# Four of the thirteen transfers of each half of the query stack, issued from ScalarE's queue in the steady rounds

## The reference, cut to what matters

```
q = split_heads(x @ w_q);  k, v = split_heads(text @ w_k), split_heads(text @ w_v)
k_ip, v_ip = split_heads(ip_h @ w_k_ip), split_heads(ip_h @ w_v_ip)
out = softmax(q k^T / sqrt(32)) v + softmax(q k_ip^T / sqrt(32) + mask_ip) v_ip
result = merge_heads(out) @ w_out + b_out + x
```

## Time and profile before

| what | value |
|---|---|
| median of three runs | 734.93 us (734.69 to 735.64) |
| profiled execution | 729.49 us |
| its span, first to last instruction | 727.7 us |
| TensorE busy | 688.1 us, 95% |
| VectorE busy | 540.1 us, 74% |
| ScalarE busy | 288.3 us, 40% |
| GpSimd busy | 213.5 us, 29% |
| transfers on SyncE's queue | 88.45 MB, 44.7% of 16 engines' span |
| transfers on ScalarE's queue | 0.61 MB, 0.4% |
| granted TensorE clock, mean | 0.979 of full speed |

### The profile page before, as it was taken

One profiled execution on the slowest core, in us unless ns is written; L12 is line 12 of the kernel. 1 busy time (PEld: TensorE's weight loads), 2 busy tenths in 40 slices (PEclk: granted clock), 3 DMA queues, 4 the chain that ended last, 5 costly groups with the idle time before them and its releaser, 6 DMA issues.

```text
span 727.7 us, 18922 instructions
## 1 busy us (share of the span) xinstructions
PE 688.1 (95%) x6410; PEld 628.2 (86%) x6410; DVE 540.1 (74%) x1686; ACT 288.3 (40%) x626; POOL 213.5 (29%) x359
## 2 busy tenths in 40 slices
PE   4979778999999999999999999999999999999987
PEld 3567467989999998989999999999999989899876
DVE  5341539878787979797878788787879797978764
ACT  1031117153534435261617162535444261617061
POOL 7100004324150504142423324151505042423223
PEclk9879999999999999999999999999999999999979
DMA  9935954253434444433435263534344444434310
GB/s 266 323 98 137 267 147 121 66 155 92 136 90 134 102 127 103 140 89 102 130 89 156 68 163 82 147 96 127 98 127 103 133 96 125 104 92 114 90 49 37
DMA packets 79543, 89.52 MB, mean 123 GB/s; under 512 B 10680, under 2 KB 63416, under 8 KB 79492
## 3 DMA queue, kind: packets, MB, share of 16 engines
q1 hardware_dynamic: 79016, 88.45, 44.7%
q10 hardware_dynamic: 492, 0.61, 0.4%
HBM read 39.21 MB, written 10.62 MB: 68 GB/s over the span
## 4 chain that ended last, share of the span: by engine, by line
PE 75%; DMA 8%; DVE 7%; SPq 6%; issue 2%; ACT 1%; ACTq 0%; POOL 0%; DVEq 0%
PE psum L1019 32%; PE psum L1124 9%; PE psum L1076 7%; PE psum L1108 6%; PE psum L1103 5%; DMA q_stack<-aux_a 4%; SPq L457 3%; PE psum L1132 3%; PE psum L901 3%; PE psum L1133 2%; SPq L429 2%; DMA wo_raw<-in_L_xattn_w_v_ip 2%; PE psum L1147 2%; PE psum L980 2%; PE psum L1130 1%
## 5 line engine op out<-in xcount | busy, mean ns | idle before, releaser
L522 POOL TENSOR_TENSOR attn<-o_parts 128x128 f32<-128x128 f32 x160 | 73.8, 461 | 418.9 <-DVE o_parts L844 418.9
L803 DVE TENSOR_REDUCE neg_max<-psum 128x2 f32<-128x292 f32 x320 | 144.7, 452 | 64.0 <-PE psum L1076 63.4
L1019 PE MATMUL psum<-wo_both,at_hi 128*128 128x320 f32 x640 | 153.2, 313 | 0.0
L1019 PE MATMUL psum<-xt_hi,wq_hi 128*128 128x256 f32 x400 | 114.9, 287 | 1.4 <-DVE xt_lo L773 1.4
L1076 PE MATMUL psum<-k_stack,q_stack 104*128 104x154 f32 x640 | 112.6, 286 | 3.5 <-DVE neg_max L804 1.5
L1019 PE MATMUL psum<-xt_hi,wq_lo 128*128 128x256 f32 x400 | 112.1, 280 | 0.0
L1019 PE MATMUL psum<-xt_lo,wq_hi 128*128 128x256 f32 x400 | 112.0, 280 | 0.0
L831 DVE TENSOR_TENSOR p_lo<-psum,p_hi 128x512 f16<-128x512 f32 x160 | 107.9, 682 | 2.8 <-ACT psum L657 2.8
L1019 PEld LDWEIGHTS psum<-wo_both,at_hi 128*128 128x128 f32 x640 | 109.6, 188 | 0.0
L655 ACT ACTIVATE p_hi<-psum 128x512 f16<-128x512 f32 x160 | 95.3, 595 | 27.8 <-PE psum L1103 27.7
L1124 PE MATMUL psum<-v_tail,p_tail 128*128 128x264 f32 x320 | 102.0, 400 | 2.6 <-DVE p_lo L831 1.6
(11 more groups left out here) (93 smaller groups left out, 1260.3 us busy)
## 6 DMA issues: line engine op xcount, KB each, us to landing
q_stack<-q_hi SPq DMA_DIRECT2D x128, 96.0 KB
x_in<-in_x SPq DMA_DIRECT2D x16, 640.0 KB, 4.1
x_res<-in_x SPq DMA_DIRECT2D x16, 640.0 KB, 5.1
out<-out_sb SPq DMA_DIRECT2D x32, 320.0 KB
q_stack<-q_hi SPq DMA_DIRECT2D x128, 64.0 KB
q_stack<-q_lo SPq DMA_DIRECT2D x64, 96.0 KB
q_stack<-q_lo SPq DMA_DIRECT2D x64, 64.0 KB
q_stack<-aux_a SPq DMA_DIRECT2D x48, 64.0 KB, 2.4
```

The costliest lines, as they stand in the source:

```text
L522: nc.gpsimd.tensor_tensor(cols, o_parts[:, qt, 0:4, :], o_parts[:, qt, 4:8, :], ALU.add).then_inc(att_half, 1)
L803: nc.vector.tensor_reduce(dst[:, :, 0], src[:, :, 0:TEXT], AX_X, ALU.max, negate=True)
L1019: last = nc.tensor.matmul(ps, l(c), r(c), start=(i == 0), stop=(i == len(terms) - 1))
```

## The change

The four transfers of the first part of each half (rows 0 to 31, the high part) leave SyncE's block and are issued from ScalarE's queue in all rounds that have a BACK stage. In ScalarE's list the block for set A comes behind ST(2,1) and ahead of Q3, the one for set B behind Q4 and ahead of AT(0,0). The other nine transfers stay with SyncE. All count on the same semaphore as before. In round 0 SyncE issues all thirteen.

```diff
 ACT_STEPS = [
...
-    (BACK, "ST", 2, 1), (FRONT, "Q", 3), (BACK, "ST", 3, 0), (BACK, "ST", 3, 2), (BACK, "ST", 3, 1),
-    (BACK, "ST", 4, 0), (BACK, "ST", 4, 1), (BACK, "ST", 4, 2), (FRONT, "Q", 4), (BACK, "AT", 0, 0), (NEXT, "X", 0),
+    (BACK, "ST", 2, 1), (FRONT, "STK", 0), (FRONT, "Q", 3), (BACK, "ST", 3, 0), (BACK, "ST", 3, 2), (BACK, "ST", 3, 1),
+    (BACK, "ST", 4, 0), (BACK, "ST", 4, 1), (BACK, "ST", 4, 2), (FRONT, "Q", 4), (FRONT, "STK", 1), (BACK, "AT", 0, 0),
+    (NEXT, "X", 0),
...
+        def queries_to_stack(queue, n, row, part):
+
+            groups = (SET_A, SET_B)[n]
+            g0, g1 = groups[0], groups[-1] + 1
+            src = q_hi if part == "hi" else q_lo
+            for j in range(4):
+                queue.dma_start(q_stack[row:row + DH, 4 * g0 + j:4 * g1:4, :].bitcast(F32),
+                                src[DH * j:DH * (j + 1), g0:g1, :].bitcast(F32)).then_inc(stack_in[n], 16)
...
-                        for row, part in STACK_PARTS:
-                            src = q_hi if part == "hi" else q_lo
-                            for j in range(4):
-                                sp.dma_start(q_stack[row:row + DH, 4 * g0 + j:4 * g1:4, :].bitcast(F32),
-                                             src[DH * j:DH * (j + 1), g0:g1, :].bitcast(F32)).then_inc(stack_in[n], 16)
+                        for row, part in STACK_PARTS[1:] if it.back else STACK_PARTS:
+                            queries_to_stack(sp, n, row, part)
...
+                    if kind == "STK":
+                        n = args[0]
+                        groups = (SET_A, SET_B)[n]
+
+                        act.wait_ge(qh_done, t * GROUPS + groups[-1] + 1)
+                        act.wait_ge(st_ready, t * ST_ALL - ST_ALL + 1 + max(ST_TURN[(g, u)] for g in groups for u in range(3)))
+                        queries_to_stack(act, n, *STACK_PARTS[0])
```

## The result

The changed kernel took 760.6 us (median of 4 runs, 756.0 to 764.4) against 734.8 us for the kernel before in the same comparison (4 runs, 733.0 to 735.6): ratio 1.037, 95% interval 1.031 to 1.042. It is slower, as forecast, but by 25.8 us where the sum said 14.5, and 0.6 us beyond the top of the range. The profiled execution took 759.7 us, its span is 757.9 us.

A forecast was written before the change was run, and what follows sets the result against it. TensorE was taken to bound the kernel, busy 38.50 of 38.80 us per steady round. Stalls of 11.76 + 0.62 + 0.95 + 0.71 + 0.50 = 14.5 us on the 734.93 us median gave 749 us, range 736 to 760.

The forecast's parts named there:

- the sum: Whole run: steady rounds 11.76 us, rounds 1, 8 and 15 0.62, 0.95 and 0.71, plus 0.50: 14.5 us slower.
- block 1: Set B's four ScalarE issues between Q4 and AT(0,0): wait for Q4's result, stall S(1,0,0) by 0.98 us per steady round.
- signs: Steady rounds: AT(0,0) starts 3.0 us after Q4, TensorE idles about 1 us ahead of S(1,0,0), mask waits gone.
- block 0: Set A's four ScalarE issues ahead of Q3: 2.51 us, Q3 delayed 0 to 0.15 us, covered by 0.64 us slack.
- the threshold: Between Q4 and AT(0,0) on ScalarE: the stall of S(1,0,0) begins at 0.35 us per issue.
- the price of block 1 in the sum: Behind Q4: four issues at 597 ns, 2.51 us, plus 0.05 us wait and register work; S(1,0,0) 0.98 us late.
- The price of an issue beside another queue's: SyncE and ScalarE issuing at once: larger ratio 1.7 gives 1.02 us per issue; 597 ns was taken instead.
- (B): Rival: SyncE and ScalarE issuing at once slow each other, 1.02 us per issue, 789 us, or 769 us; chance 0.10.
- (D): Rival: earlier stack arrival makes timed runs faster, about 730 us, if ScalarE issues stay under 0.35 us; chance 0.11.
- (C): Rival: no change, 735 us; ScalarE issues of 0.3 to 0.4 us fit the gap, stack not waited for; chance 0.11.

The follow-up runs named there:

- Two issues: Kernel before with only set B's block on ScalarE, two of its four transfers there and the others on SyncE: 734.3 us, ratio 1.000.
- three of 1.99 us: Kernel before with only set B's block on ScalarE, three of its four transfers there and ten on SyncE: 743.8 us, ratio 1.015.
- the late place: Changed kernel with set B's four issues moved from behind Q4 to behind AT(1,1), ahead of X2: 734.0 us, ratio 1.000.
- the filled kernels: Changed kernel with nine needless products on TensorE ahead of S(1,0,0), timed twice: 752.5 us, ratio 1.026; then 753.4 us, ratio 1.027.
- the second comparison: Changed kernel timed again beside its version with nine needless products ahead of S(1,0,0): 758.9 us (ratio 1.033) and 753.4 us (1.027).
- block 0 alone: Kernel before with only set A's four transfers issued from ScalarE, set B's thirteen staying on SyncE: 734.1 us, ratio 1.002.

## Why the prediction was right or wrong

**Right: the mechanism, its place and its sign.** TensorE bounds the rounds, an earlier stack is worth nothing there, block 1 waits for ScalarE's own last result and holds the queue, and the delay passes through at_hi, at_lo and the maxima to S(1,0,0). Each piece stands in the chain after, and moving block 1 removed all of the cost. Of the signs that it named, AT(0,0) starts 3.17 us after Q4's activation (3.0 said) and TensorE idles 1.03 us ahead of S(1,0,0), put down to the maxima (1 said).

**Right in the result, wrong in size: block 0 is hidden.** The sequencer issued it while the queue's exponentials ran. The step under-priced it (2.91 us measured, 2.51 said) and made Q3 at most 0.15 us late; it was 0.5 us late. The 0.64 us of slack that the step had found still covered that, with little to spare.

**Right: the threshold.** The working says that the stall begins at 0.35 us per issue, 1.4 us for the block. Two issues of 1.24 us in all cost nothing, three of 1.99 us cost 10.7 us.

**Wrong in size: the price of block 1 in the sum.** The step took four issues at 597 ns, 2.51 us; they took 2.64 us. By itself this queue took 2.59 us for them in the late place, so most of the excess is that ScalarE's issues are a little longer than SyncE's, and 0.05 us comes from issuing beside it. The register operation and the hand-over behind them took 0.11 us, not 0.05. S(1,0,0) was 1.20 us late rather than 0.98, and a touched round 1.35 us longer; the other 0.15 us arises behind S(1,0,0), in the filled kernels too, and its cause wasn't looked for. Fifteen rounds at 1.35 us are 20.2 us, and the two filled kernels, which have the delay without the clock's falls, are 19.4 and 20.2 us above the kernel before, where the sum said 14.5. That alone would be 755 us, inside the range.

**Wrong by omission: "the sum" has no term for TensorE's clock.** It priced a stall at its length. A stall in an engine that otherwise hardly idles also put its clock at risk: 5.5 to 6.4 us in the medians, 1.5 us for each round in which it happened. The rows of the kernel before that could have warned are those of round 1 shown above, 3.8 us nearly idle and then 3.4 us at 1.2 GHz; the rounds behind it had one gap of 0.72 us, in round 2, and none else above 0.25 us to learn from. This term took the time past the top of the range. How far past is chance: the second comparison had 758.9 us, below the 760 of the range, with the same two errors in it.

**A row misread, and a premise.** The price of an issue beside another queue's rested on 368 ns for SyncE "by itself". It wasn't: ScalarE's issue of line 572 ran at 31.90 us, SyncE's of line 377 at 31.89. The ratio of 1.7 and the 1.02 us of (B) have no basis in that row. And (D) laid the 5.4 us between the profiled execution and the others to the touched rounds. The table of the thirteen rounds speaks against it: with block 0 alone the profiled execution was 3.2 us longer than the one before, and 2.9 us of that lay ahead of round 2. By its own figures (D)'s stall and gain would cancel at 0.44 us per issue, not 0.42.

**The rivals.** (B), two queues slowing each other, was real in kind, on ScalarE's side at least, and small in size: 622 ns in the median of 120 issues on ScalarE, nearly all beside one of SyncE's, not 1.02 us.

```profile
L367 SPq DMA_DIRECT2D q_stack<-q_lo x128: 585/598/1035, 64.7 to 704.7; - x128
L367 ACTq DMA_DIRECT2D q_stack<-q_hi x120: 592/622/994, 120.3 to 704.4; - x120
```

(C) and (D) needed issues under 0.4 us; none on ScalarE's queue was under 0.592. The Trainium skill (DMA: Bandwidth & Descriptors, Issuing engines are not separate DMA queues) says that spreading the issue saves only the sequencer's time. The runs agree: nothing was gained. It calls that time usually small beside the transfer itself, which says nothing on whether it is small beside the gap of the queue that receives it: here 1.4 us to spare, and 2.6 us put in.

One sentence of the section on the kernel says that only a transfer can bring the heads behind one another. No run here tried another way, so take it as what this kernel does.

## What to carry to other kernels

An issue of one of these transfers costs its queue 0.6 us though the profile doesn't call the engine busy, so look for room in the gap ahead of the next instruction that somebody waits for, and at whether the issue must first wait for the instruction ahead of it: four such transfers cost nothing ahead of Q3, and block 1's four cost nothing behind AT(1,1) but about 20 us (26 with the clock) behind Q4. Before filling a stall with other work, list what else waits for the same late engine. And a stall in the bounding engine is to be priced with its clock, as a range, not by its length alone.

## What the runs showed of the hardware that I had not expected

- A stretch of 1.2 us in which TensorE was busy for only 0.27 us, in rounds otherwise full, was followed by some 3 us mostly at 1.2 GHz in 2 of fourteen rounds of one execution; another execution had 6 such rounds. With the stretch filled there was none in two profiles. With three transfers, where TensorE idled 0.37 us, there was none in one.
- An issue on ScalarE's queue takes longer beside SyncE's than alone: 0.84 us against 0.59 to 0.62 us in one round of the kernel with block 1 late. Whether SyncE's slow too isn't clear: with block 0 alone they took 0.59 to 0.86 us beside ScalarE's, and 0.83 us just after those had ended.
- ScalarE's sequencer issued a transfer 1.2 us before the last activation queued ahead of it started (470.69 and 471.88 us above).
